# Two row strips of 64, two token tiles in one go, biases seeded in PSUM, and quantised x summed by GpSimd from transposed parts

## The reference

```
attn = einsum('ds,td->st', w1, w2) * sparse_mask          # 1024 x 1024, nonzero near the diagonal
xn   = layernorm(x)
y    = gelu(einsum('bds,st->bdt', xn, attn) + b2, approximate=False)
x_q  = clip(xn * x_scale).astype(float8_e5m2)             # x_scale = 57344 / max|xn|
w_q  = clip(weight * w_scale).astype(float8_e4m3fn)
f    = (x_q @ w_q.T) / x_scale / w_scale + bias
out  = x + y + f
```

## Times and profile before

| | us |
|---|---|
| median of 3 runs (lowest, highest) | 293.36 (292.41, 294.8) |
| the profiled execution | 293.77 |
| its span, first to last instruction | 292.0 |
| busy in the span: PE, DVE, ACT, POOL | 251.1, 208.8, 203.0, 205.7 |
| DMA queue of SP, share of 16 engines' time | 91.2% |
| mean granted TensorE clock | 0.97 |

### The profile page before, as it was taken

How to read it: one execution, slowest core, us unless ns; L and a number is a source line. 1 busy time by engine, 2 the same in 40 slices (tenths; PEclk the granted TensorE clock), 3 DMA queues, 4 the chain that set the end, 5 groups by cost and what they waited for, 6 DMA issues and landing times.

```text
span 292.0 us, 4911 instructions
## 1 busy us (share of the span) xinstructions
PE 251.1 (86%) x1818; PEld 175.2 (60%) x1818; DVE 208.8 (72%) x225; ACT 203.0 (70%) x239; POOL 205.7 (70%) x137
## 2 busy tenths in 40 slices
PE   0039699990279799999999999999999999999994
PEld 0039688880278366666666656666666666666661
DVE  3888999999997457956659575567746766656563
ACT  1079979999996698676676749667588687772210
POOL 2000499999997189996978786887789897776333
PEclk9999999997559999999999999999999999999999
DMA  6999999999999239999999999999999989879913
GB/s 235 415 411 410 409 407 410 407 384 408 313 226 142 45 69 198 227 216 224 220 216 229 232 192 251 224 226 215 216 240 209 215 222 214 213 203 225 202 72 147
DMA packets 99721, 72.56 MB, mean 249 GB/s; under 512 B 85488, under 2 KB 87280, under 8 KB 99696
## 3 DMA queue, kind: packets, MB, share of 16 engines
q1 hardware_dynamic: 99696, 72.24, 91.2%
HBM read 34.60 MB, written 16.78 MB: 176 GB/s over the span
## 4 chain that ended last, share of the span: by engine, by line
PE 43%; DMA 21%; ACT 10%; SPq 8%; POOL 7%; issue 6%; DVE 4%; ACTq 0%; POOLq 0%; DVEq 0%
PE psF L1054 12%; PE psT L1054 11%; DMA x_all<-in_L_attn_x_dram 8%; PE psY L1037 8%; PE psZ L1037 8%; DMA home<-home 8%; DMA x_all<-in_L_attn_w_dram 4%; POOL x_all L532 3%; SPq L362 3%; POOL home L494 2%; ACT squares L567 2%; PE psT L970 2%; ACT xq L670 2%; PE psY L980 2%; ACT junk L554 2%
## 5 line engine op out<-in xcount | busy, mean ns | idle before, releaser
L532 POOL TENSOR_TENSOR x_all<-x_all,biases 128x1024 f32<-128x1024 f32 x32 | 75.5, 2361 | 35.0 <-DVE x_all L894 35.0
L494 POOL TENSOR_TENSOR home<-home 128x1024 f16<-128x1024 f32 x32 | 68.3, 2133 | 8.6 <-ACT home L663 8.0
L1054 PE MATMUL psT<-wqT,wq_nat 128*128 128x512 f16 x256 | 57.9, 379 | 1.4 <-ACT wq_nat L677 1.4
L1054 PE MATMUL psF<-wqT,wq_nat 128*128 128x512 f16 x256 | 57.9, 379 | 0.0
L663 ACT ACTIVATE home<-home 128x1024 f16<-128x1024 f32 x28 | 29.6, 1057 | 40.3 <-DMA home<-home 40.2
L894 DVE TENSOR_TENSOR x_all<-psZ,x_all 128x1024 f32<-128x1024 f32 x16 | 19.6, 1225 | 36.1 <-ACT psZ L682 36.1
L1037 PE MATMUL psY<-split,home 128*128 128x197 f16 (+2 forms) x480 | 44.2, 249 | 0.1
L1037 PE MATMUL psZ<-split,home 128*128 128x197 f16 (+2 forms) x480 | 44.2, 249 | 0.0
L1037 PEld LDWEIGHTS psY<-split,home 128*128 128x128 f16 x480 | 38.4, 97 | 7.4 <-DMA home<-home 0.6
L1037 PEld LDWEIGHTS psZ<-split,home 128*128 128x128 f16 x480 | 38.4, 97 | 7.1 <-DMA home<-home 0.3
L1054 PEld LDWEIGHTS psT<-wqT,wq_nat 128*128 128x128 fp8e5 x256 | 24.7, 98 | 28.5 <-issue 1.8
(11 more groups left out here) (96 smaller groups left out, 316.7 us busy)
## 6 DMA issues: line engine op xcount, KB each, us to landing
x_all<-in_L_attn_x_dram SPq DMA_DIRECT2D x32, 512.0 KB, 14.5
out_dram<-x_all SPq DMA_DIRECT2D x31, 512.0 KB, 3.3
x_all<-in_L_attn_w_dram SPq DMA_DIRECT2D x16, 512.0 KB, 15.2
x_all<-in_L_ffn_weight_dram SPq DMA_DIRECT2D x8, 512.0 KB, 7.6
squares<-_L_attn_sparse_mask_dram SPq DMA_DIRECT2D x2, 413.5 KB, 3.7
biases<-_L_attn_sparse_mask_dram SPq DMA_DIRECT2D x6, 133.0 KB, 10.5
squares<-_L_attn_sparse_mask_dram SPq DMA_DIRECT2D x2, 349.5 KB, 3.7
squares<-_L_attn_sparse_mask_dram SPq DMA_DIRECT2D x2, 285.5 KB, 3.4
```

Of the source, the lines that this page charges most:

```text
L494: nc.gpsimd.tensor_tensor(hl[:, q % 2, D:2 * D], xs[:, q % 2, :], hl[:, q % 2, 0:D], ALU.subtract).then_inc(xl_ready, 1)
L532: nc.gpsimd.tensor_tensor(x_all[:, SLOT[q], :], x_all[:, SLOT[q], :], bias_bc, ALU.add)\
L1054: ins = nc.tensor.matmul(ps_f[q % 2][:, HALF * h:HALF * h + HALF], quantised(q % XQ_RING)[:, k // 2, k % 2, :], wqT[:, k, HALF * h:HALF * ...
```

## The change

1. **Row strips.** `attention(a)` handles tiles a and a+1 together. Each 128-row block is split into two strips of 64 rows; a strip's matmul uses only its 64 rows of the array (`tile_position`), and only the columns that these 64 rows reach: 200 in place of 266 for an inner block (the reach is 68 in place of 69). Each strip walks over the four PSUM banks (two tiles, two halves) in the order of `TURNS`, so the strips are never in one bank at once; at its third and fourth turn a strip waits for the other (`strip_done`). A tile takes 60 matmuls of at most 200 columns (30 per strip, three of them of 4 columns) in place of 30.
2. **Order by pairs.** PE: ffn(a), ffn(a+1), attention(a+2). The other engines also go by pairs.
3. **Biases in PSUM.** From tile 4 on ACT `seed_y` copies a scaled b2 into `psY`/`psZ` ahead of the banded product, and the GELU applies the scale; DVE `add_b2` stays for tiles 0 to 3. From tile 2 on DVE `seed_f` copies a scaled bias into `psT`/`psF` ahead of the FP8 product. POOL `add_bias` stays for tiles 0 and 1.
4. **Quantised x.** `normalise` writes x already multiplied by `x_mul`. POOL `quantise(q)` adds the two transposed f16 parts in `hlT` into FP8. ACT's quantising and SP's second transpose of each tile are gone. Tiles 1 to 3 are summed by DVE (`sum_parts`) and quantised by ACT.
5. **Small things.** Row sums of tiles 30 and 31 move from PE to ACT and DVE; the mask has three buffers and a ninth piece (corners of the strips), and two pieces are loaded per pair; the count is spread by a DMA in the middle of the run; rows of statistics are made in ranges of 4, 4, 12 and 12 tiles.

```diff
-    for q in range(NT):                       # SP
-        if q + 2 < NT:
-            transpose_quantised(q + 2)
-        if q > 0:
-            store(q - 1)
-        if q + AHEAD < NT:
-            transpose_parts(q + AHEAD)
+    for a in PAIRS:
+        b = a + 1
+        store(a)
+        if a + AHEAD < NT:
+            transpose_parts(a + AHEAD)
+        if b < NT - 1:
+            store(b)
+        if b + AHEAD < NT:
+            transpose_parts(b + AHEAD)
...
+    def quantise(q):                          # POOL
+        wait_hlT(pool, q)
+        pool.wait_ge(f_done, q - XQ_RING + 1)
+        nc.gpsimd.tensor_tensor(quantised(q % XQ_RING), hlT[:, q % HLT_RING, 0:D],
+                                hlT[:, q % HLT_RING, D:2 * D], ALU.add, saturate=False)\
+            .then_inc(xq_ready, 1)
...
-    for q in range(NT):
-        add_bias(q)
-        if q + AHEAD < NT:
-            pool.wait_ge(xh_ready, q + AHEAD - FIRST + 1)
-            low(q + AHEAD)
+    for a in PAIRS:
+        for q in (a + 2, a + 3):
+            if FIRST <= q < NT:
+                quantise(q)
+        for q in (a + AHEAD, a + AHEAD + 1):
+            if q < NT:
+                pool.wait_ge(xh_ready, q - FIRST + 1)
+                low(q)
...
+    for a in PAIRS:                           # ACT
+        gelu(a)
+        gelu(a + 1)
+        for q in (a + 2, a + 3):
+            if FIRST <= q < NT:
+                seed_y(q)
+        for q in (a, a + 1):
+            if q + AHEAD < NT:
+                normalise(q + AHEAD)
+                high(q + AHEAD)
...
+TURNS = ("0.1.", "1.0.", ".0.1", ".1.0")      # PE: bank by bank, the strip of each turn
+    begins = not todo[r]
+    if begins:
+        todo[r] = share(r, h)
+        if n >= 2:
+            pe.wait_ge(strip_done[1 - r], STEPS * (a // 2) + n - 1)
+    b, lo, hi, part, A = todo[r].pop(0)
+    rows = slice(SROWS * r, SROWS * r + SROWS)
+    ins = nc.tensor.matmul(ps_y[q % 2][:, lo:hi],
+                           hlT[rows, q % HLT_RING, part + P * b:part + P * b + P],
+                           A[rows, at:at + hi - lo], start=begins and n < 2 and q < FIRST,
+                           stop=not todo[r], skip_group_check=True, tile_position=(SROWS * r, 0))
```

More of the change, by code:

```diff
@@ L28, with reach @@
 BAND = OFF[KB]
+def reach(b, r):
+    row = P * b + SROWS * r
+    return 0 if b == 0 else row - REACH, D if b == KB - 1 else row + SROWS + REACH
 LN_EPS = 1e-5
@@ L66, with last_turns @@
 WQ_RING, SQ_RING, XQ_RING, HLT_RING = 4, 3, 4, 4
+TURNS = ("0.1.", "1.0.", ".0.1", ".1.0")
+STEPS = len(TURNS[0])
+def last_turns(q):
+    ends = []
+    for h in range(2):
+        turns = TURNS[2 * (q % 2) + h]
+        n = max(i for i, turn in enumerate(turns) if turn != ".")
+        ends.append((int(turns[n]), STEPS * (q // 2) + n + 1))
+    return ends
 def sparse_linear_plus_fp8_linear(
@@ L305, in wait_hlT, with wait_xq, wait_y @@
             eng.wait_ge(hlT_loaded[q % HLT_RING], 16 * (q // HLT_RING + 1))
+        def wait_xq(eng, q):
+            eng.wait_ge(xq_first if q < FIRST else xq_ready, q + 1 if q < FIRST else q - FIRST + 1)
+        def wait_y(eng, q):
+            for r, n in last_turns(q):
+                eng.wait_ge(strip_done[r], n)
         @block.sync
@@ L648, in _ @@
             square(28)
+            row_sum(30)
             copy_wq(7)
@@ new lines, in _ @@
+            nc.vector.tensor_scalar(f_mul, x_inv, inv_ws, 1.0 / XSCALE, ALU.mult, ALU.mult)
+            nc.vector.tensor_scalar(y_mul, a_inv, x_inv, 1.0 / XSCALE, ALU.mult, ALU.mult).then_inc(y_scale, 1)
+            dve.wait_ge(x_scale, 1)
+            nc.vector.tensor_scalar(f_inv, x_mul, ws, XSCALE, ALU.mult, ALU.mult).then_inc(f_scale, 1)
+            then(nc.vector.tensor_scalar(b2_mul, a_mul, x_mul, XSCALE, ALU.mult, ALU.mult))
+            add_b2(1)
+            sum_parts(2)
+            for a in PAIRS:
+                b = a + 1
+                if 0 < a < FIRST:
+                    add_b2(a)
+                    add_b2(b)
+                if 1 < b and b - 1 <= KB:
+                    count_mask(b - 1)
+                add_gelu(a)
+                add_gelu(b)
+                if a == 0:
+                    count_mask(0)
+                dve.wait_ge(f_done, a + 1)
+                if b < NT - 1:
+                    add_product(a)
+                    if b < NT - 1:
+                        seed_f(a + 2)
+                    if a == 0:
+                        nc.vector.tensor_scalar(b2_seed[:, :], b2_bc, b2_mul, None, ALU.mult).then_inc(b2_scaled, 1)
+                        sum_parts(3)
+                        count_mask(1)
+                    if b > 1 and b <= KB:
+                        count_mask(b)
+                    dve.wait_ge(f_done, b + 1)
+                    add_product(b)
+                    seed_f(b + 2)
+                if b == KB + 1:
+                    dve.wait_ge(mask_counted, KB + 1)
+                    nc.vector.tensor_reduce(off_cnt, cnt[:, :], AX_X, ALU.add).then_inc(off_ready, 1)
+                if a == SPREAD_AT + 2:
+                    dve.wait_ge(off_loaded, 16)
+                    then(nc.vector.tensor_reduce(off_any[0:1, :], off_row[:, :], AX_X, ALU.add))
+                    nc.vector.tensor_scalar(flag[0:1, :], off_any[0:1, :], 0.5, None, ALU.is_gt).then_inc(flag_ready, 1)
@@ L1043, in ffn, with share @@
[L1043 to L1051 removed]
+            def share(r, h):
+                cut = [(b, max(lo, 0, HALF * h), min(hi, D, HALF * h + HALF))
+                       for b in range(KB) for lo, hi in [reach(b, r)]]
+                return [(b, lo, hi, part, A) for b, lo, hi in cut if lo < hi
+                        for part, A in ((0, Ah), (0, Al), (D, Ah))]
@@ new lines, in attention @@
+            def attention(a):
+                for q in (a, a + 1):
+                    wait_hlT(pe, q)
+                    if q >= FIRST:
+                        pe.wait_ge(y_seeded, q - FIRST + 1)
+                    elif q >= 2:
+                        pe.wait_ge(u_ready, q - 1)
+                spent, step, todo = [0] * NS, [0] * NS, [[] for _ in range(NS)]
+                while min(step) < STEPS:
+                    r = min((r for r in range(NS) if step[r] < STEPS), key=lambda r: spent[r])
+                    n = step[r]
+                    bank = next(i for i in range(len(TURNS)) if TURNS[i][n] == str(r))
+                    q, h = a + bank // 2, bank % 2
+                    begins = not todo[r]
[5 more added lines that the diff above has]
+                    rows = slice(SROWS * r, SROWS * r + SROWS)
+                    at = OFF[b] + lo - C0[b]
+                    ins = nc.tensor.matmul(ps_y[q % 2][:, lo:hi],
+                                           hlT[rows, q % HLT_RING, part + P * b:part + P * b + P],
+                                           A[rows, at:at + hi - lo], start=begins and n < 2 and q < FIRST, stop=not todo[r],
+                                           skip_group_check=True, tile_position=(SROWS * r, 0))
+                    spent[r] += hi - lo + 8
+                    if not todo[r]:
+                        ins.then_inc(strip_done[r], 1)
+                        step[r] += 1
@@ L1114, in _ @@
                                                   identF[:, :])
-                    for k in range(KB):
-                        ins = nc.tensor.transpose(psF[:, P * k:P * k + P],
-                                                  pairs(g_xs, k // 2, k % 2), identF[:, :])
                     ins.then_inc(g_x_transposed, 1)
```

321 lines of the change are left out of this document (161 added, 160 removed).

## The result

The changed kernel takes 304.61 us (median of 4 runs, 303.77 to 307.25), the kernel before 294.08 in the runs beside it: a ratio of 1.038 with an interval of 1.029 to 1.046. It is slower by 10.5 us. 310 was forecast, with a range of 292 to 322.

A forecast was written before the change was run, and what follows sets the result against it. A closed loop of waits through GpSimd and the DMA queue was taken as the bound: 133 + 12 x 13.4 + 4.1 + 6.9 + 4.1 = 308.9 us of span, plus 1.8, giving 310 us; 8-in-10 range 292 to 322.

The forecast's parts named there:

- TensorE: Second stage: strips run at the same time, banded product 4.1 us per pair, 11.0 with FP8 products in place of 12.1.
- the estimate of 0.36: Cost on TensorE of two changes of tiling mode per pair, each estimated at a matmul's tail of 0.18 us.
- The long rival: Banded product: strips run one after the other (337 us), or issue at 87 ns limits them (365 us); chance 0.08.
- The 62 ns: Sequencer's pace per matmul in one decoding mode; by it the banded pair takes 7.4 us, the time about 325.
- GpSimd's sum: Adding two transposed f16 parts of a tile on GpSimd, not in the earlier trace, taken as 2.13 us.
- the bound of 1.19: Lower bound in us for GpSimd's sum, as a one-input operation costs; the time would be 295 us, chance 0.13.
- The closed loop: Second stage: sum, low part, transpose, store, second transpose wait on each other in a ring; 13.4 us per pair.
- store and second transpose: DMA queue in the loop: store lands 1.8 us after the first transpose, second transpose 2.5 us after the store.
- The term for fetches: Fetches of instructions that stall the loop's DMA part, about 1.1 us each; 0.4 us taken per turn.
- The start: VectorE's chain of 21.7 us, then other engines and transposes; tile 7 lands at about 133 us, 6 us lost.
- the clock: TensorE's granted clock was assumed to stay at 1.00 through idle gaps, cost nothing; a risk only at longer gaps.
- Rival 2: Steady part: the loop turns in under 11.0 us, so TensorE binds at 11.2 per pair; 282 us, chance 0.13.

The follow-up runs named there:

- e12: Changed kernel with both transposes of a pair issued ahead of both stores and the banded product without strips, as before the change: 298.0 us.
- e2: Changed kernel with SyncE issuing both transposes of a pair ahead of both stores, GpSimd's order kept: 288.8 us, 0.983 of the kernel before.
- e4: Changed kernel with GpSimd's sum of the second tile of each pair made twice, once into an unread scratch tile: 329.7 us.
- e5: Changed kernel with GpSimd's sum of the first tile of each pair made twice, once into an unread scratch tile: 308.5 us.
- e3: Changed kernel with the strips undone, 30 banded matmuls of 128 rows per tile as before the change: 306.7 us.
- e7: Changed kernel with 24 in place of 6 warming matmuls before TensorE waits for the scale of x: 305.8 us.
- e1: Changed kernel with GpSimd making the two low parts of a pair ahead of the two sums: 298.9 us.
- e6: Kernel before with only the row strips added, one tile at a time, halves exchanged between strips: 295.9 us, 1.006 of the kernel before.

## Why the prediction was right, and where it was off

**TensorE: right, 0.2 us a pair too low.** 120 banded matmuls took 4.18 us (4.1 forecast). That is 18336 columns, 4.4 per ns where the kernel before had 2.3, so the strips do run at the same time. By the Trainium skill, "TensorE: Matmul & The Clock Gate", Part 3, matmuls in different row groups run concurrently; the trace agrees. e12 and e2 put a price on all of it without the loop: 12.07 - 11.27 = 0.8 per pair, not 1.1. 5.11 of banded product became 4.20, and 0.1 went to the second FP8 product, 3.55 (200.70 to 204.25 in e2) in place of 3.45. By the Trainium skill, "TensorEngine Tiling (Array Packing)", Key Properties, a change of tiling mode drains the engine. The trace fits a small cost of this kind: 0.1 to 0.2 per pair, and not the estimate of 0.36. That the change of mode is the reason of the 0.1 wasn't tested. The long rival (337 or 365) is out: load and matmul follow each other every 35 ns over 120 pairs. The 62 ns that I quoted from the Trainium skill ("TensorE: Matmul & The Clock Gate", "Wait — 56ns, not 53.3ns?") as the sequencer's pace in one decoding mode don't bind here.

**GpSimd's sum: right.** 2.129 us measured for 2.13; the bound of 1.19 for narrow inputs is out.

**The closed loop: right as a mechanism, its length over by 0.7 us on the mean.** Place, members and order are as forecast, and e4, e5, e3 and e2 each confirm one part of it. Its turn was mis-sized:

| term | forecast | measured |
|---|---|---|
| sum and low part | 4.26 | 4.2 |
| first transpose | 4.2 | 4.3 |
| store and second transpose | 1.8 + 2.5 | 3.9 |
| hand-overs | 0.2 | under 0.1 |
| slower landings (forecast as fetches of instructions) | 0.4 | 0 in nine turns, 0.3 to 0.7 in three: 0.1 on the mean |
| turn | 13.4 | 12.5, mean 12.7 |

The store and the second transpose were taken from a queue that never ran empty; here the landings are 0.4 closer. The term for fetches was mis-sized by 0.3. Their number did rise, from 15 to 22, but a turn of 12.5 has one as well. The three slower turns (issues of the first transpose at 138.65, 176.94 and 240.14; 13.2, 13.0 and 12.9 us) have two each, and they alone have a first transpose that lands after 4.7 to 4.9 us in place of 4.3. In the rates there is the gap of the earlier trace rows, some 1 us of almost nothing. The turn from 177 us and an ordinary one, GB/s in 40 slices of 177 to 190 and of 202.6 to 215.2:

```profile
GB/s 0 0 0 143 209 94 5 9 22 287 290 290 291 427 441 340 315 195 221 217 220 217 216 217 210 404 416 403 403 0 0 0 0 0 0 0 0 0 50 0
```

```profile
GB/s 0 0 0 67 222 211 211 219 217 219 200 386 416 338 247 379 133 215 221 220 215 219 216 203 215 286 377 403 403 0 0 0 52 0 0 0 0 0 0 0
```

So the mechanism of the term is there, three times in twelve and at 0.3 to 0.7 of the turn; that the fetch causes the gap is argued from this company alone. One first transpose ahead of the loop (125.48) landed after 4.9 us with a single fetch, and one in e7 after 5.4. GpSimd's range of deviations, 3.3 us of work in the turn from 177 us, isn't the reason: behind it GpSimd still waited 0.99 us for the second landing. Twelve turns at 0.73 too much are 8.8 us.

**The start: right in kind, 1.4 us short up to tile 7's landing, for reasons that I had at nothing.** Tile 7 landed at 134.38 (133 forecast). I priced two sums of parts at 1.4 together, without a row for it; an undisturbed one takes 1.21 to 1.23, and one of them took 2.65, beside GpSimd's bias add. And I priced the clock at nothing: after the 2.95 us of idling ahead of tile 4 the granted clock was 0.50 from 122 to 124 us, and the banded pair took 5.64 where others take 4.18. That held up a sum of GpSimd, which waited 2.75 us for an FP8 product until 130.41. In the loop's own gaps of 1.2 to 1.9 us the clock stayed at 1.00, as assumed; that was partly luck, since gaps hardly longer in other runs did not leave it there (last section).

**In sum:** 133 + 12 x 13.4 + 15.1 was forecast for the span; 134.6 + 12 x 12.67 + 15.4 = 302.0 is what it was, from the first banded product behind tile 7's landing. Errors of unlike sign, the loop's (-8.8), the start's (+1.6) and the end's (+0.3), make the span 6.9 shorter than forecast; the median fell short by 5.4. That the total is so near owes something to errors that cancel. Rival 2, by which TensorE binds once the second transpose isn't held up by a store, was a fair description of another kernel: it is e2, and its steady turn is 11.2 as worked out there. Its time of 282 left out the losses at the start, which e2 keeps: 288.8.

What stays open: what else makes up the 3.9 us at the start, why single transposes land later, and whether a start without sums of parts on VectorE would bring e2 below 285. None was tried.

## What to carry to other kernels

Write down, for each in-order queue, what stands behind a wait, and follow it until it comes back to itself; a ring of such waits has a period that no busy share shows, and saving work beside it brings next to nothing (e3) while one reordered DMA issue brings 16 us (e2). When an engine's list is reordered to break one ring, look for the ring that the new order closes (e1). Halves of a change can each be worth nothing (e6, e12) and together be worth something (e2).
